# Scores in two buffers, masks half a row ahead, the transposed adjacency kept packed, x kept on chip

## The chip, the cores and the metric

The kernel runs on one core of a Trainium2 chip. TensorE (PE in the profile) multiplies and transposes, VectorE (DVE), ScalarE (ACT) and GpSimd (POOL) work elementwise, SyncE (SP) issues the transfers. The metric is the device time of one execution in microseconds.

## The reference

N = 4096 nodes, D = 128 features, `adj` is a 4096 x 4096 matrix of zeros and ones.

```python
deg = clip(adj.sum(axis=1), 1.0); dis = deg ** (-0.5)
diffusion = (dis[:, None] * adj * dis[None, :]) @ x - x
norms = maximum(norm(x, axis=-1), 1e-8)
sim = x @ x.T / (norms[:, None] * norms[None, :])
attn = softmax(beta * sim * adj, axis=1)
l0 = diffusion + sigmoid(alpha) * (attn @ x - x)
x = layernorm(x + l0)
x = layernorm(x + relu(adj @ (x @ weights)))
```

## The kernel before

All node indices are cut into R = 32 row blocks of 128 ("rows" below), and each row into C = 4 pieces of 1024 columns or H = 8 pieces of 512 columns ("steps" h = 0 to 7).

The attention stage handles one row after another. For row r, with q = r % 2:

- SP loads the row's adjacency in four pieces of 512 KB into `land`, which has two buffers (line 230). ACT casts each piece to bytes in `adj_bytes[q]`, with the row sums beside it (`cast`, line 369). The piece i is scaled by 64 >> i, so that POOL can add the four pieces into one `packed` block (`pack`, lines 287 to 293). PE turns it (`turn_adj`, line 838), and DVE takes it apart again by a shift and an AND, four instructions a row, into the row's transposed adjacency `adjT` of 128 KB a partition (`store_adj`, line 581).
- PE computes a row's cosines, three matmuls of 512 columns a step (`cosines`, line 853), into the two banks of `ps_s`. DVE multiplies them by the mask and writes `scores` (`mask`, line 593), with maxima beside it; `row_max` (lines 602, 604) makes the bias of the exponential. ACT computes the exponentials in place in four pieces (`exps`, line 401).
- PE turns the exponentials, four transposes a step, into one of four banks of `ps_e` (`turn_e`, line 864). ACT writes the high half in float16 (`e_high`, line 408), DVE the rest (`e_low`, line 608). PE multiplies both by x (`attend`, lines 877, 879), in `ps_acc`. DVE adds the finished row to `u` by two linked instructions (`attn_add`, lines 615, 618), after which `attend(r + 1, 0)` may start.

`scores` has one buffer. A mask of row r + 1 may be written at step h only once `turn_e(r, h)` has read it, so the masks of row r + 1 run beside the steps of row r, the last one at its step 7, and `row_max(r + 1)` and the exponentials of row r + 1 come after it. The order on each engine is written out by hand: on PE a step of row r is `turn_e(r, h)`, `attend(r, h - 3)`, `cosines(r + 1, h + 1)`, and the last three attends of a row stand behind its step 7, one of them in the next row. On DVE a step is `mask(r + 1, h)`, `e_low(r, h)`, then one of four `store_adj`, and `attn_add(r - 1)` stands at h = 2.

Between the stages x is loaded a second time from memory (line 247), POOL scales it by `dis` into `y` (lines 335, 339), and DVE writes the low halves (`y_low`, line 686).

The second stage has two layers of 32 rows. A row is 32 matmuls of 256 columns (line 918) with the transposed adjacency as weights, into one of four banks of `ps_e`. Rows 0 to 3 read `adjT` itself; the other rows read one of two buffers in `adj_bytes`, which `stage_block` fills two rows ahead by one copy of 128 x 1024 words (line 682). In layer 0, DVE's `step(r)` waits for the row's matmuls and then runs `stage_block`, `head0` (725, 728, 719, 721), `xw_low(r - 5)` (756) and `normalise(r - 1)` (745, 750). ACT's `step` runs `xw_high(r - 5)` (464), `turned_out(r - 4)` (458, 460) and `root(r)` (453), in that order. PE's `whole_row(r)` has `turn_x1(r - 4)` (924) in its middle and `x1_w(r - 4)` (929) behind it; the latter waits for line 460. Layer 1 has `head1` (735, 738) and `normalise` in its place, and no product with the weights.

## Time and profile before

| | us |
|---|---|
| median of 3 runs | 761.27 (760.44 to 761.53) |
| span of the profiled execution | 757.8 |
| attention stage and what stands ahead of it, until the first matmul of layer 0 | 518.17 |
| last matmul of layer 0 to the end | about 119 |

The profile is of one execution; its own device time is not stated, only its span, which lies 3.5 us below the median of the runs. The span begins with the first instruction. Durations in it overlap a little: an instruction of VectorE is shown some 0.08 us longer than the distance to the next one.

### The profile page before, as it was taken

How to read it: one execution, taken by the hardware profiler on the slowest of the kernel's cores; microseconds unless marked ns; L12 is line 12 of the kernel's file. 1: busy time of each engine (PE TensorE's matmuls, PEld its weight loads, DVE VectorE, ACT ScalarE, POOL GpSimd, SP SyncE). 2: the span in 40 equal slices, each digit the busy share in tenths (PEclk: the TensorE clock that was granted, in tenths of full speed). 3: DMA queues.
4: the chain of work that ended last, by engine and by line, in shares of the span. 5: the costliest groups of instructions: out<-in, count | busy, mean ns of one | idle time of the engine just before them, and what ended most of it. 6: DMA issues, size and time to landing. Idle time of an engine off the chain costs nothing. (4 is left out here: it accounts for less than half of the span.)

```text
span 757.8 us, 19379 instructions
## 1 busy us (share of the span) xinstructions
PE 721.4 (95%) x6163; PEld 578.5 (76%) x6163; DVE 572.1 (75%) x1644; ACT 494.4 (65%) x1001; POOL 128.7 (17%) x161
## 2 busy tenths in 40 slices
PE   6889989999999999999999999989999999999997
PEld 6567767777777777777777777768999998888886
DVE  4878878887888788878887888797566666465655
ACT  5888899889988998899889988982122223211111
POOL 2781112111211121112111211170000000000000
PEclk9999999999999999999999999999999999999999
DMA  5645543455445534553445345510000000000000
GB/s 177 189 139 143 159 132 124 127 152 160 115 129 151 160 114 131 150 159 115 130 150 159 115 131 149 169 51 5 1 0 0 0 0 0 12 17 14 28 14 28
DMA packets 22502, 73.81 MB, mean 97 GB/s; under 512 B 2640, under 2 KB 3152, under 8 KB 22480
## 3 DMA queue, kind: packets, MB, share of 16 engines
q1 hardware_dynamic: 22480, 73.54, 32.5%
q8 instruction: 11, 0.18, 0.1%
q14 instruction: 11, 0.09, 0.0%
HBM read 71.44 MB, written 2.10 MB: 97 GB/s over the span
## 5 line engine op out<-in xcount | busy, mean ns | idle before, releaser
L593 DVE CUSTOM_DVE_ANT_1 scores<-ps_s,adj_bytes 128x512 f32<-128x512 f32 x252 | 172.5, 685 | 72.7 <-PE ps_e L864 67.8
L853 PE MATMUL ps_s<-xn_parts,xn_signed 128*128 128x512 f16 x756 | 204.4, 380 | 1.7 <-DVE cmax L593 1.7
L877 PE MATMUL ps_acc<-x_parts,eT_parts 128*128 128x256 f16 x1024 | 192.8, 272 | 4.6 <-DVE u L618 2.0
L879 PE MATMUL ps_acc<-x_parts,eT_parts 128*128 128x128 f16 x1024 | 180.9, 219 | 0.0
L608 DVE SCALAR_TENSOR_TENSOR eT_parts<-ps_e,eT_parts 128x512 f16<-128x512 f32 x256 | 175.2, 685 | 3.7 <-ACT eT_parts L408 3.1
L864 PEld LDWEIGHTS ps_e<-ident,scores 128*128 128x128 f32 x1024 | 123.0, 141 | 69.7 <-issue 27.6
L408 ACT ACTIVATE eT_parts<-ps_e 128x512 f16<-128x512 f32 x256 | 147.0, 587 | 37.3 <-PE ps_e L864 36.6
L864 PE MATMUL ps_e<-ident,scores 128*128 128x128 f32 x1024 | 150.1, 274 | 18.4 <-ACT scores L401 18.4
L401 ACT ACTIVATE scores<-scores,col 128x1024 f32<-128x1024 f32 x128 | 157.6, 1231 | 1.1 <-DVE col L604 1.1
L369 ACT ACTIVATE adj_bytes<-land 128x1024 uint8<-128x1024 f32 x128 | 135.2, 1057 | 23.3 <-DMA land<-in_adj 22.7
L877 PEld LDWEIGHTS ps_acc<-x_parts,eT_parts 128*128 128x128 f16 x1024 | 100.0, 98 | 24.0 <-issue 9.6
L918 PE MATMUL ps_e<-xn_parts,adj_bytes 128*128 128x256 f16 x896 | 105.4, 273 | 0.0
L879 PEld LDWEIGHTS ps_acc<-x_parts,eT_parts 128*128 128x128 f16 x1024 | 100.1, 98 | 5.3
L918 PE MATMUL ps_e<-x_parts,adj_bytes 128*128 128x256 f16 x896 | 98.0, 273 | 0.0
L918 PEld LDWEIGHTS ps_e<-x_parts,adj_bytes 128*128 128x128 fp8e4 x896 | 87.7, 98 | 10.1
L918 PEld LDWEIGHTS ps_e<-xn_parts,adj_bytes 128*128 128x128 fp8e4 x896 | 87.7, 98 | 9.5
L853 PEld LDWEIGHTS ps_s<-xn_parts,xn_signed 128*128 128x128 f16 x756 | 60.2, 98 | 42.5 <-issue 2.1
L287 POOL TENSOR_TENSOR packed<-adj_bytes 128x256 uint32<-128x256 uint32 x32 | 23.3, 728 | 357.9 <-PE ps_at L838 357.9
L453 ACT ACTIVATE col<-mv,col 128x1 f32<-128x1 f32 x64 | 18.6, 291 | 97.7 <-DVE mv L721 97.7
L682 DVE COPY adj_bytes<-adjT 128x1024 uint32 (+1 forms) x56 | 38.8, 693 | 50.2 <-PE ps_e L918 50.2
L487 ACT ACTIVATE scores<-ps_e,col 128x128 f32<-128x128 f32 x32 | 11.8, 369 | 88.9 <-PE ps_e L918 88.9
L581 DVE TENSOR_SCALAR adjT<-ps_at 128x256 uint32 (+1 forms) x128 | 52.6, 413 | 0.0
(113 smaller groups left out, 570.1 us busy)
## 6 DMA issues: line engine op xcount, KB each, us to landing
land<-in_adj SPq DMA_DIRECT2D x128, 512.0 KB, 3.6
u<-in_x SPq DMA_DIRECT2D x4, 512.0 KB, 8.0
out<-u SPq DMA_DIRECT2D x7, 256.0 KB, 2.0
land<-in_x SPq DMA_DIRECT2D x2, 512.0 KB, 3.3
adj_bytes<-in_x SPq DMA_DIRECT2D x2, 512.0 KB, 3.8
out<-u SPq DMA_DIRECT2D x1, 192.0 KB, 1.9
eT_parts<-in_L_gnn_weights SPq DMA_DIRECT2D x1, 64.0 KB, 9.0
scores<-in_L_gnn_weights SPq DMA_DIRECT2D x1, 64.0 KB, 1.7
```

Of the source, the lines that this page charges most:

```text
L369: nc.scalar.activation(adj_bytes[:, q, i * CH:(i + 1) * CH], land[:, i % 2, :], ACT.Copy, scale=float(BYTE_ONE >> i), accum_out=deg[:, i, ...
L401: nc.scalar.activation(scores[:, i * CH:(i + 1) * CH], scores[:, i * CH:(i + 1) * CH], ACT.Exp, bias=neg_max, scale=abs_beta, accum_out=cs ...
L408: nc.scalar.activation(eT_parts[:, h % 4, 0, :], ps_e[:, h % 4, :], ACT.Copy, scale=E_SCALE).then_inc(e_hi, 1)
L581: nc.vector.tensor_scalar(adjT_rows[:, r, i * CH // K:(i + 1) * CH // K], ps_at[:, 0:CH // K].bitcast(U32), i, BYTE_ONE * 0x01010101, ALU. ...
L593: nc.vector.tensor_tensor_reduce(scores[:, o:o + BANK].rearrange("p (k q) -> p k q", k=K), score_bank(h, start).rearrange("p (k q) -> p k ...
L608: nc.vector.scalar_tensor_tensor(eT_parts[:, h % 4, 1, :], ps_e[:, h % 4, :], E_SCALE, eT_parts[:, h % 4, 0, :], ALU.mult, ALU.subtract).t ...
L682: nc.vector.tensor_copy(stage[q], adjT_rows[:, r, :]).then_inc(staged, 1)
L853: ins = nc.tensor.matmul(score_bank(h, start), xn_signed[:, q, part, :], xn_parts[:, other, o:o + BANK], start=(part == 0 and other == 0), ...
L864: ins = nc.tensor.transpose(ps_e[:, h % 4, n * P:(n + 1) * P], scores[:, t * P:(t + 1) * P], ident[:, :])
L877: nc.tensor.matmul(ps_acc[:, 0:2 * D], eT_parts[:, h % 4, 0, n * P:(n + 1) * P], x_parts[:, t, :], start=(t == 0), stop=(t == R - 1), skip ...
L879: ins = nc.tensor.matmul(ps_acc[:, 0:D], eT_parts[:, h % 4, 1, n * P:(n + 1) * P], x_parts[:, t, 0:D], start=False, stop=(t == R - 1), ski ...
L918: return nc.tensor.matmul(ps_e[:, n, 0:2 * D], lhs[:, b, :, k], y[t], start=(t == 0), stop=(t == R - 1))
```

## The change

- `scores`, `cmax`, `csum`, `neg_max` and `packed` get two buffers, `land` four.
- The masks of a row are made half a row earlier: steps 0 to 3 of row r make the masks 4 to 7 of row r + 1, with `row_max(r + 1)` at step 3, and steps 4 to 7 make the masks 0 to 3 of row r + 2. The cosines move with them, and in a step they stand ahead of `attend`. ACT makes the casts of row r + 2 in steps 0 to 3 and the exponentials of row r + 1 in steps 4 to 7. `attn_add(r - 1)` moves to h = 3. The last three attends of a row stand in steps 0 to 2 of the next.
- `store_adj` is one copy of the packed block into `packT`. `stage_block` takes the blocks apart in the second stage, by four instructions of 128 x 256 words a row, four rows ahead into a `stage` with four buffers, and now for all 64 rows.
- x is kept in `x_keep`; the second load is gone.

```diff
-        adjT = sb("adjT", [P, R, B, P], U32)
-        land = sb("land", [P, 2, CH], F32)
+        packT = sb("packT", [P, R, CH // K], U32)
+        stage = sb("stage", [P, G, N // K], U32)
+        land = sb("land", [P, C, CH], F32)
+        x_keep = sb("x_keep", [P, R, D], F32)
-        scores = sb("scores", [P, N], F32)
+        scores = sb("scores", [P, 2, N], F32)
...
-                sp.dma_start(x_again_at[q].rearrange("p (b k) d -> p b (k d)", b=2),
-                             x_v[:, 2 * q:2 * q + 2, :]).then_inc(x_again[q], 16)
...
             def row(r, q, start=False):
-                casts = (4, 5, 6, 7) if start else (3, 4, 6, 7)
-                exps(r, 0)
-                exps(r, 1)
...
+                for h in range(C):
                     e_high(r, h, start)
+                    cast(r + 2, q, h)
+                for h in range(C, H):
+                    e_high(r, h, start)
+                    exps(r + 1, 1 - q, h - C)
+
+            exps(0, 0, 0)
+            cast(1, 1, 2, first=True)
+            exps(0, 0, 1)
+            exps(0, 0, 2)
+            cast(1, 1, 3, first=True)
+            exps(0, 0, 3)
             row(0, 0, start=True)
...
+            def store_adj(r):
+
+                dve.wait_ge(adj_turned, r + 1)
+                nc.vector.tensor_copy(packT[:, r, :], ps_at[:, 0:CH // K].bitcast(U32)).then_inc(adj_stored, 1)
...
                 if not start:
-                    dve.wait_ge(e_turned, r * H + (h + 1 - H))
+                    dve.wait_ge(e_turned, r * H + (h + 1 - 2 * H))
...
-                    if h == 2 and not start:
+                    if h == 3 and not start:
                         if second:
                             dve.wait_ge(u_init, C)
                         attn_add(r - 1)
-                    mask(r + 1, 1 - q, h)
-                    if h == H - 1:
-                        row_max(r + 1)
+                    if h < C:
+                        mask(r + 1, 1 - q, h + C, start)
+                    elif not degrees:
+                        mask(r + 2, q, h - C)
+                    if h == C - 1:
+                        row_max(r + 1, 1 - q)
                     e_low(r, h)
-                    if h >= 4:
-                        store_adj(r, h - 4)
+                    if h == C:
+                        store_adj(r)
...
-                nc.vector.tensor_copy(stage[q], adjT_rows[:, r, :]).then_inc(staged, 1)
+            def stage_block(k, r, n):
+                for i in range(C):
+                    nc.vector.tensor_scalar(stage[:, n, i * CH // K:(i + 1) * CH // K], packT[:, r, :], i,
+                                            BYTE_ONE * 0x01010101, ALU.logical_shift_left,
+                                            ALU.bitwise_and).then_inc(staged, 1)
...
             for h in range(H):
-                if h == 2:
+                if h == 3:
                     attn_add(R - 2)
...
                 e_low(R - 1, h)
+                if h < C:
+                    stage_block(h, h, h)
+                if h >= C:
+                    y_low(h - C)
+                if h == C:
+                    store_adj(R - 1)
...
-            def step(r, n, lag, more=True):
+            def step(r, n, lag, ahead):
                 dve.wait_ge(rows_done, r + 1)
-                if lag >= G and more:
-                    stage_block(r + 2, n % 2)
+                stage_block(r + G, ahead, n)
                 head0(r, n)
...
-                step(r, r % G, 5, r + 2 < R)
-                if r + 2 >= R:
-                    stage_block(G + r + 2 - R, r % 2)
+                step(r, r % G, 5, r + G - R)
...
                 for h in range(H):
-                    turn_e(r, h, start)
+                    turn_e(r, q, h, start)
                     if h == 2:
-                        turn_adj(r, start)
+                        turn_adj(r, q, start)
+                    if h < C and left >= 1:
+                        cosines(r + 1, 1 - q, h + C)
+                    elif h >= C and left >= 2:
+                        cosines(r + 2, q, h - C)
                     if h >= LAG:
                         attend(r, h - LAG, start)
-                    elif h == 1 and not start:
-                        attend(r - 1, H - 1)
-                    if left and 1 <= h < H - 1:
-                        cosines(r + 1, 1 - q, h + 1)
-                for h in range(H - LAG, H - 1):
-                    attend(r, h, start)
-                    if left > 1:
-                        cosines(r + 2, q, h - (H - LAG))
+                    elif not start:
+                        attend(r - 1, h + H - LAG, second)
...
-                pe.wait_ge(staged, r + (layer * (R - G) - G + 1))
+                pe.wait_ge(staged, r * C + (layer * R * C + C))
```

## Rows read from the trace of the kernel before

**Rows 1.** The page, part 1: busy us (share of the span) x instructions.

```profile
PE 721.4 (95%) x6163; PEld 578.5 (76%) x6163; DVE 572.1 (75%) x1644; ACT 494.4 (65%) x1001; POOL 128.7 (17%) x161
```

**Rows 2.** Waits, 100 to 480 us: who waited for what: us, times, longest.

```profile
PEld ps_e L864 <- issue: 23.2, 25, 1.0
```

**Rows 3.** Timeline of VectorE: two of the 32 row maxima (start, us).

```profile
77.65 0.16 DVE L602 TENSOR_REDUCE col<-cmax 128x1 f32<-128x8 f32 x1
...
488.14 0.16 DVE L602 TENSOR_REDUCE col<-cmax 128x1 f32<-128x8 f32 x1
```

**Rows 4.** Timeline, 302.9 to 304.7 us: one step of PE, and ACT behind its transposes.

```profile
302.94 0.60 PE L864 MATMUL ps_e<-ident,scores 128*128 128x128 f32 x4
...
303.37 0.27 PE L877 MATMUL ps_acc<-x_parts,eT_parts 128*128 128x256 f16 x1
...
303.57 0.60 ACT L408 ACTIVATE eT_parts<-ps_e 128x512 f16<-128x512 f32 x1 [1.15 <-PE ps_e L864]
...
304.03 0.81 PE L853 MATMUL ps_s<-xn_parts,xn_signed 128*128 128x512 f16 x3
...
304.68 0.60 PE L864 MATMUL ps_e<-ident,scores 128*128 128x128 f32 x4
```

**Rows 5.** Timeline, 312 to 314 us: the sum of a row, and the attend behind it.

```profile
312.40 0.34 DVE L615 SCALAR_TENSOR_TENSOR u<-ps_acc,col,u 128x128 f32 x1
...
313.28 0.27 PE L877 MATMUL ps_acc<-x_parts,eT_parts 128*128 128x256 f16 x1
```

**Rows 6.** Timeline of ACT, about 300 to 310 us: high half, cast, exponential.

```profile
300.25 0.59 ACT L408 ACTIVATE eT_parts<-ps_e 128x512 f16<-128x512 f32 x1
...
300.73 1.05 ACT L369 ACTIVATE adj_bytes<-land 128x1024 uint8<-128x1024 f32 x1
...
308.76 1.23 ACT L401 ACTIVATE scores<-scores,col 128x1024 f32<-128x1024 f32 x1
```

**Rows 7.** Timeline of VectorE, 300 to 302 us: mask, low half.

```profile
300.45 0.68 DVE L593 CUSTOM_DVE_ANT_1 scores<-ps_s,adj_bytes 128x512 f32<-128x512 f32 x1
...
301.06 0.68 DVE L608 SCALAR_TENSOR_TENSOR eT_parts<-ps_e,eT_parts 128x512 f16<-128x512 f32 x1
```

**Rows 8.** Timeline: the first exponential, and the first matmul of attend(1, 0).

```profile
31.75 1.24 ACT L401 ACTIVATE scores<-scores,col 128x1024 f32<-128x1024 f32 x1 [0.31 <-DVE col L604]
```

```profile
54.20 0.27 PE L877 MATMUL ps_acc<-x_parts,eT_parts 128*128 128x256 f16 x1
```

**Rows 9.** The chain that ended last, the piece that begins layer 0.

```profile
518.17 15.83 PE ps_e L918 x145
```

**Rows 10.** Groups by line and form: table loads of ACT: busy us, mean ns.

```profile
L441 ACT ACT_TABLE_LOAD x2 | 2.6, 1283 | 0.0
```

**Rows 11.** Timeline of VectorE, 517 to 522 us: low half of y, four stores, two copies.

```profile
517.20 1.21 DVE L686 TENSOR_TENSOR xn_parts<-adj_bytes,xn_parts 128x1024 f16<-128x1024 f32 x1
...
518.98 1.41 DVE L581 TENSOR_SCALAR adjT<-ps_at 128x256 uint32<-128x256 uint32 x4
520.30 1.28 DVE L682 COPY adj_bytes<-adjT 128x1024 uint32<-128x1024 uint32 x2
```

**Rows 12.** Groups of VectorE by form: operations with pointers to scalars.

```profile
L604 DVE TENSOR_SCALAR col<-col 128x1 f32<-128x1 f32 x32 | 6.9, 214 | 1.1
...
L750 DVE TENSOR_SCALAR scores<-u,mv,rstd 128x128 f32<-128x128 f32 x12 | 4.2, 346 | 0.4
```

**Rows 13.** Waits of the whole span, in front of the copies of stage_block.

```profile
DVE adj_bytes L682 <- PE ps_e L918: 50.2, 52, 1.8
```

**Rows 14.** Timeline, 578 to 582 us: a row of layer 0.

```profile
578.00 0.69 DVE L682 COPY adj_bytes<-adjT 128x1024 uint32 x1 [0.93 <-PE ps_e L918]
...
581.04 0.27 ACT L460 ACTIVATE scores<-ps_s 128x128 f32<-128x128 f32 x1
...
581.50 0.39 PE L929 MATMUL ps_acc<-scores 128*128 128x128 f32 x2
```

**Rows 15.** Timeline, behind the last row of layer 0.

```profile
641.51 0.49 PE L929 MATMUL ps_acc<-scores 128*128 128x128 f32 x2 [0.27 <-ACT scores L460]
```

More of the change, by code:

```diff
@@ L99, in two_layer_gnn @@
         alpha_c, beta_c, e_alpha, sigma, u_scale, abs_beta = (c(n) for n in range(6))
-        neg_max, total, r_total, gain = (c(n) for n in range(6, 10))
+        neg_max = [c(6), c(29)]
+        total, r_total, gain = (c(n) for n in range(7, 10))
         attn_scale, x_up, dif_scale, w_up, w_down, eps_c = (c(n) for n in range(10, 16))
@@ L118, in two_layer_gnn @@
         w_loaded = sem("w_loaded")
[L119 to L120 removed]
+        land_full = [sem(f"land_full{i}") for i in range(C)]
         ident_zero = sem("ident_zero")
@@ L394, in _, with exps, e_high @@
             cast(1, 1, 1, first=True)
-            cast(1, 1, 2, first=True)
-            def exps(r, i):
+            def exps(r, q, i):
                 if i == 0:
                     act.wait_ge(max_done, r + 1)
-                nc.scalar.activation(scores[:, i * CH:(i + 1) * CH], scores[:, i * CH:(i + 1) * CH], ACT.Exp,
-                                     bias=neg_max, scale=abs_beta, accum_out=csum[:, i:i + 1]).then_inc(exp_done, 1)
-            def e_high(r, h, start):
+                piece = scores[:, q, i * CH:(i + 1) * CH]
+                nc.scalar.activation(piece, piece, ACT.Exp, bias=neg_max[q], scale=abs_beta,
+                                     accum_out=csum[:, q, i:i + 1]).then_inc(exp_done, 1)
+            def e_high(r, h, start=False):
                 act.wait_ge(e_turned, r * H + (h + 1))
@@ L447, in _ @@
                 row(r + 1, 1)
-            late_row(R - 2, 0)
-            late_row(R - 1, 1)
+            e_high(R - 2, 0)
+            e_high(R - 2, 1)
+            e_high(R - 2, 2)
+            act.wait_ge(deg_done, 1)
+            nc.scalar.activation(dis[:, :], dis[:, :], ACT.Sqrt).then_inc(deg_root, 1)
+            e_high(R - 2, 3)
+            nc.scalar.activation(table_loads[1], eps_c, ACT.Exp)
+            for h in range(C, H):
+                e_high(R - 2, h)
+                exps(R - 1, 1, h - C)
+            for h in range(H):
+                e_high(R - 1, h)
+                if h == 0:
+                    nc.scalar.activation(table_loads[2], eps_c, ACT.Sqrt)
             def root(r, q, base):
@@ L648, in _ @@
                                          ALU.mult, ALU.mult))
+            for h in range(C):
+                mask(1, 1, h, start=True)
             def row(r, q, start=False, second=False, degrees=False):
@@ L855, in cosines, with turn_e @@
                 ins.then_inc(s_done, 1)
-            def turn_e(r, h, start=False):
+            def turn_e(r, q, h, start=False):
                 if h % 2 == 0:
@@ L904, in _ @@
                 cosines(0, 0, h, start=True)
-            cosines(1, 1, 0)
-            cosines(1, 1, 1)
+            for h in range(C):
+                cosines(1, 1, h)
             row(0, 0, start=True)
-            row(1, 1)
+            row(1, 1, second=True)
             with pe.Fori(2, R - 3, 2) as r:
@@ L913, in _ @@
             row(R - 1, 1, left=0)
-            attend(R - 1, H - 1)
+            for h in range(H - LAG, H):
+                attend(R - 1, h)
             def add_tile(n, lhs, t, y):
```

204 lines of the change are left out of this document (78 added, 126 removed).

## The prediction

> **What bounds the kernel now.** I read the page first: PE is busy for 95% of the span [rows 1], and the chain that ended last consists of its matmuls in the second stage. That share says little of the attention stage, so I read next how long one of its rows takes. The maxima of 27 rows lie 410.5 us apart, 15.20 us a row [rows 3]. A step in which PE never stands takes 1.74 us: 0.43 for four transposes, 0.66 for eight attend matmuls, 0.65 for three cosines [rows 4]. Eight steps and the two transposes of the packed block (0.22, at a fourth of 0.43 each) make 14.14 us. So PE stands idle for 1.06 us in each row, and nearly all of that can be named. At the start of a row the weight loads of `turn_e` wait 0.93 us (23.2 over 25 rows, [rows 2]), because the exponentials cannot start before the last mask has been written. The rest lies mostly ahead of `attend(r, 0)`, behind `attn_add`. The second stage is PE's without holes: VectorE waits for PE 0.97 us in front of each staging copy [rows 13].
>
> **Scores in two buffers, masks and cosines half a row earlier.** The same instructions run, in another order, so only waits can change. The wait at the row's start goes: `exps(r + 1, 0)` now stands in step 4 of row r, and the transposes that need it are four steps later.
>
> Can ACT follow? In steps 4 to 7 it has a high half (0.48) and an exponential (1.23), 1.71 us against PE's 1.74; in steps 0 to 3 a high half and a cast, 1.53 us [rows 6, 4]. That makes 12.96 us of 14.14, just enough. The casts find their data: with four `land` buffers a piece is ordered a whole row ahead, and POOL packs long before.
>
> What is late next is `attn_add`, now at h = 3. I count from the start s2 of step 2. The cosines start behind six transposes, at s2 + 0.65, and their result is there after 0.81 and a few hundredths [rows 4], at s2 + 1.50. VectorE runs the mask (0.61) and the low half (0.60) [rows 7], until s2 + 2.71, and only then `attn_add`. From its first instruction to the attend behind it 0.88 us pass [rows 5]: `attend(r, 0)` can start at s2 + 3.59. PE gets to it at s2 + 1.96 + 0.43 + 0.65 = s2 + 3.04. So it waits 0.55 us in each row, and behind it on PE's queue everything else waits. Row: 14.14 + 0.55 = **14.69 us**, 0.51 less than now. Elsewhere VectorE has room: eight masks and low halves are 9.7 us [rows 7], the small instructions about 2.
>
> **Start.** ACT used to interleave the first row's exponentials with high halves. Now it does four exponentials and two casts first, from 31.75 [rows 8]: 4 x 1.23 + 2 x 1.05 = 7.0, so the first high half starts at 38.75. Four steps at 1.53 and four at 1.71 follow, 13.0 us, and row 1 begins on ACT at 51.7. The third high half of row 1 ends 3 x 0.48 + 2 x 1.05 later, at 55.2, its low half at 55.8, then `attn_add(0)`, and `attend(1, 0)` at 56.7, where it is at 54.20 now [rows 8]. That costs 2.5 us. This `attend` lies 7.07 us behind the start of its row (three steps with the 0.22, 1.08, the stall), so row 1 starts at 49.6 as PE sees it, and row 30 at 49.6 + 29 x 14.69 = 475.6.
>
> **Rows 30 and 31.** They lose cosines and masks, so PE is not the bound. In row 30 ACT passes its two table loads (1.3 us each with 0.2 of work, [rows 10]), starts the fifth high half at 8.7 (PE's step 4 begins at 8.1, and ACT follows 0.63 later, [rows 4]), and takes four times 1.71: row 31's first high half ends at 16.0. A third load: the second one ends at 18.0. From there VectorE bounds, as it carries the new staging and `y_low`: seven low halves 4.2, `attn_add` 0.76, three `y_low` at 1.13 (the next instruction overlaps the 1.21 by 0.08, [rows 11]) 3.4, the store and two small ones 0.6, and 12 staging instructions of pace p. Then PE's last attend, 0.8 with its signal. Layer 0 starts 27.8 + 12p behind row 30's start. The second load of x is off this path in either case: POOL needs some 13 us for y from the ninth microsecond of row 30 on, and `y_low(0)` comes at 24.
>
> **The pace p** is what the trace does not show: a shift and an AND from SBUF to SBUF. Bounds: the same operation from PSUM, four in 1.41 us, hence 0.33 apart [rows 11]; and the copy, which moves 1024 words in 0.69 us, faster than one word a cycle would allow (L686 needs 1.21 us for as many), and whose 0.59 pace for 1024 words gives 0.20 for 256 if the length-dependent 0.53 shrinks to 0.13 [rows 11]. The pointer operations speak for the slow end [rows 12]: one pointer and one element take 214 ns, two pointers and 128 elements 346, a full cycle for each element unless the second pointer costs 66 ns itself. I take 0.20, since source, target and number of inputs are the copy's, and keep 0.33. With it layer 0 starts at 475.6 + 30.2 = 505.8; with 0.33 at 507.4. Now it starts at 518.17 [rows 9]. Gain 12.4 or 10.8.
>
> The Trainium skill, VectorE: DVE Perf Modes, section "The TRN2 errata", speaks against cutting one copy into four: each instruction that reads SBUF pays a fixed cost, given as 58 cycles beside the elements. By its formula, an estimate, the copy costs 0.59 and four parts 0.78 at two elements a cycle, nearly my 0.80. Its tier table has tensor_scalar at two elements a cycle for fp32 in SBUF; rows 12 don't settle that for this operation.
>
> **Layer 0.** Staging takes 0.80 in place of 0.61, d = 0.19 (or 1.33, d = 0.72), at the head of VectorE's step. Its 0.93 us of idle time [rows 14] covers that as throughput. But behind it hang the statistics, `root`, `xw_high` and `turned_out` on ACT, and `x1_w` on PE. The copy of x1t ends at 581.31 and PE uses it at 581.50 [rows 14]; in the three other rows of a loop turn there are 0.5 us. Less a signal of 0.1, the slack is 0.1 once and 0.4 three times. A stall of one row gives the next the same time back, so about half of d minus slack remains as a mean: 0.6 us in all for p = 0.20, and (0.72 - 0.35) / 2 x 27 = 4.9 us for p = 0.33.
>
> **Between the layers.** PE already waits 0.27 us for this chain [rows 15]. In steps 30 and 31 the staging stood behind the rest, now it stands ahead: 0.80 (or 1.33) us on the path.
>
> **Layer 1.** The idle time of 0.97 [rows 13] covers d, rows are staged four ahead, and nothing on PE hangs on VectorE's answer. 0. The tail behind the last matmul has no staging before or after. 0.
>
> **Sum.** -12.4 + 0.6 + 0.8 = -11.0: span 746.8. The median of the runs lies 3.5 us above the profiled span, so **750.3 us**.
>
> **Rivals.**
> - *Slow staging* (p = 0.33): -10.8 + 4.9 + 1.3 = -4.6, 756.7 us. For it: rows 12.
> - *No stall at attn_add*: if VectorE reaches it earlier than I count, 29 x 0.55 = 16 us less, 734.3. Against it: every link of the chain is a measured duration and stands in a fixed order on VectorE's queue.
> - *VectorE takes the second stage, slower than before*: staging instructions with addresses from registers may not overlap at all. At the unoverlapped PSUM duration of 0.41 each, d is 1.04: last row 2.6 dearer (gain 9.8), layer 0 (1.04 - 0.32) / 2 x 27 = 9.7, between the layers 1.7, layer 1 0.06 x 27 = 1.6: +3.2, 764.5 us. It decides from p = 0.38 on, and at 0.5 VectorE alone would set both layers' rows.
> - *The new order gives nothing*: something I don't see (ACT, with 0.03 us to spare in a step) fills the row up to 15.20. 0.51 x 29 = 14.8 more: 765.1.
>
> **How the numbers follow.** Forecast 0.50, slow staging 0.23, no stall 0.09, VectorE-bound 0.12, nothing gained 0.06. The forecast's own range is 746 to 755 (0.1 us a row in the stall, 2 us at the start). The likeliest time is 750.3. The range runs from 738, between forecast and no stall, to 762, which holds slow staging and leaves out the two slow cases. A measurement tells 0.2%, 1.5 us, from no change. Slow staging may reach into that, so faster 0.80, same 0.07, slower 0.13.
>
> **What would show it.** Row maxima 14.7 us apart; PE's wait at a row's start gone and one of 0.55 ahead of `attend(r, 0)`, released by `attn_add`'s second instruction; `attend(1, 0)` at 56.7; layer 0 from about 506; staging instructions 0.20 apart and 0.29 long; PE waiting for x1t in layer 0 seldom, and 1.1 us between the layers. The forecast is wrong if the staging pace is 0.3 or more, or if rows are 14.2 or over 15.

## The result and the profile after

| | before | after |
|---|---|---|
| median of the runs, us | 760.34 (18 runs) | 762.27 (18 runs, 761.7 to 764.2) |
| span of the profiled execution, us | 757.8 | 760.1 |
| first matmul of layer 0, us | 518.17 | 518.50 |
| from there to the end, us | 239.6 | 241.6 |

The ratio is 1.003, with a 95% interval of 1.0021 to 1.0038: the change makes the kernel a little slower. The forecast was 750.3 us, with a range up to 762, and 11.0 us less span; 2.3 more came. The end of the attention stage hardly moved, so the missing gain has to be looked for there, row by row.

Each run with a span on record is 1.8 us longer than that span. The 3.5 us between span and median in the forecast were then these 1.8 and, an estimate, 1.7 by which the profiled execution was quicker than the median of three. So the spans miss the forecast by 13.3 us and the medians by 12.0; below, spans are compared.

Timeline of VectorE of the kernel after, three neighbouring row maxima (columns here and below: start us, duration us, engine, line, operation, out<-in, xcount, and in brackets the idle time before and who ended it; the lines that answer to [rows 3]):

```profile
446.62 0.16 DVE L586 TENSOR_REDUCE col<-cmax 128x1 f32<-128x8 f32 x1
...
461.66 0.16 DVE L586 TENSOR_REDUCE col<-cmax 128x1 f32<-128x8 f32 x1
...
476.70 0.16 DVE L586 TENSOR_REDUCE col<-cmax 128x1 f32<-128x8 f32 x1
```

They lie 15.04 us apart, where before had 15.20 and the forecast 14.69. In 29 rows that is 10.2 us of the 13.3 by which the forecast missed the span.

Waits of the kernel after, 100 to 480 us (who waited for whom: us in total, times, longest):

```profile
DVE scores L577 <- PE ps_s L839: 74.3, 151, 0.7
...
PE ps_acc L863 <- DVE u L602: 17.1, 26, 0.7
```

The wait of the weight loads at a row's start [rows 2] is gone. In its place PE waits 0.66 us in each row for the second instruction of `attn_add`. One row of VectorE shows why, and PE's attend behind it:

```profile
307.16 0.69 DVE L592 SCALAR_TENSOR_TENSOR eT_parts<-ps_e,eT_parts 128x512 f16<-128x512 f32 x1
308.57 0.69 DVE L577 CUSTOM_DVE_ANT_1 scores<-ps_s,adj_bytes 128x512 f32<-128x512 f32 x1 [0.73 <-PE ps_s L839]
309.19 0.08 DVE L577 DVE_READ_ACCUMULATOR2_ANT cmax<- 128x1 f32 x1
309.19 0.69 DVE L592 SCALAR_TENSOR_TENSOR eT_parts<-ps_e,eT_parts 128x512 f16<-128x512 f32 x1
309.79 0.34 DVE L599 SCALAR_TENSOR_TENSOR u<-ps_acc,col,u 128x128 f32 x1
310.17 0.35 DVE L602 SCALAR_TENSOR_TENSOR u<-ps_acc,col,u 128x128 f32 x1
```

```profile
310.67 0.27 PE L863 MATMUL ps_acc<-x_parts,eT_parts 128*128 128x256 f16 x1 [0.66 <-DVE u L602]
```

The cosines of this step began at 307.44. The mask on L577 starts 1.13 us behind that, the low half on L592 0.62 later, `attn_add` 0.60 later, and the attend another 0.88: 310.67. VectorE has nothing to do for 0.73 us ahead of that mask, and then is the late one.

Timeline of the last row of the kernel after, VectorE's first three staging blocks (a block is four instructions), and POOL beside them:

```profile
500.44 3.88 DVE L670 TENSOR_SCALAR stage<-packT 128x256 uint32<-128x256 uint32 x4
...
504.83 1.20 DVE L670 TENSOR_SCALAR stage<-packT 128x256 uint32<-128x256 uint32 x4
...
506.56 0.88 DVE L670 TENSOR_SCALAR stage<-packT 128x256 uint32<-128x256 uint32 x4
```

```profile
499.12 1.90 POOL L327 TENSOR_TENSOR x_keep<-x_keep,norm_r 128x1024 f32<-128x1024 f32 x1
501.11 1.17 POOL L330 TENSOR_SCALAR xn_parts<-x_keep 128x1024 f16<-128x1024 f32 x1
502.24 1.92 POOL L327 TENSOR_TENSOR x_keep<-x_keep,norm_r 128x1024 f32<-128x1024 f32 x1
```

Four staging instructions take 0.88 us where they are alone, and 3.88 in the first block, beside POOL's work on y. One by one, the first, third and fourth instruction of that block are:

```profile
500.44 0.73 DVE L670 TENSOR_SCALAR stage<-packT 128x256 uint32<-128x256 uint32 x1
...
501.29 1.12 DVE L670 TENSOR_SCALAR stage<-packT 128x256 uint32<-128x256 uint32 x1
...
502.34 1.98 DVE L670 TENSOR_SCALAR stage<-packT 128x256 uint32<-128x256 uint32 x1
```

They end at 501.17, 502.41 and 504.32, each 0.15 us behind the end of one of POOL's three instructions (501.02, 502.28, 504.16). The one-input conversion on L330 holds VectorE up just as the two multiplications do. The low half at 499.83, whose first input is in PSUM, takes its usual 0.69 beside the first of the multiplications.

`attn_add(30)` stands behind three of these blocks on VectorE's queue, and PE waits for it for 8 us, in which the granted clock falls:

```profile
508.23 0.37 PE L863 MATMUL ps_acc<-x_parts,eT_parts 128*128 128x256 f16 x1 [8.03 <-DVE u L602]
```

Table by stretch of the kernel after (stretch, length, busy us of each engine with the number of instructions, granted clock as a share of full speed, then the share of the DMA engines and GB/s):

```profile
490.00:500.00 10.00, 9.53 (x101) 8.59 (x99) 6.47 (x20) 9.74 (x18) 6.69 (x5) 1.00 0.01 2
500.00:510.00 10.00, 1.97 (x13) 1.53 (x12) 9.46 (x22) 2.69 (x5) 5.12 (x4) 0.64 0.00 0
510.00:520.00 10.00, 9.40 (x87) 8.22 (x86) 8.37 (x14) 2.39 (x4) 0.00 (x0) 0.85 0.03 8
```

The second stage is close to what was forecast. Between the layers [rows 15] became:

```profile
643.82 0.49 PE L912 MATMUL ps_acc<-scores 128*128 128x128 f32 x2 [1.08 <-ACT scores L447]
```

From the first matmul of layer 0 to this one 125.32 us pass, 123.34 before: 0.81 of the difference is the wait, and 1.17 lie in layer 0. From here to the end it is 116.3 us in both.

### The profile page after: what moved, and what is told of

It is laid out like the page before. It is cut to its first block, busy times and chain, and to the rows that moved or that the text cites. A ratio compares the mean times of both kernels' runs of the same rounds, so it can differ in the third digit from the quotient of the medians.

```text
span 760.1 us, 19535 instructions
## 1 busy us (share of the span) xinstructions
PE 716.8 (94%) x6163; PEld 577.6 (76%) x6163; DVE 568.1 (75%) x1748; ACT 499.5 (66%) x1001; POOL 128.2 (17%) x161
## 4 chain that ended last, share of the span: by engine, by line
PE 84%; DVE 9%; ACT 3%; issue 3%; DMA 1%; DVEq 0%; SPq 0%; ACTq 0%
PE ps_e L901 29%; PE ps_s L839 17%; PE ps_acc L863 14%; PE ps_e L850 12%; PE ps_acc L865 7%; DVE eT_parts L592 3%; DVE u L602 1%; DVE u L599 1%; ACT scores L392 1%; ACT adj_bytes L360 1%; DVE stage L670 1%; ACT eT_parts L399 1%; PE ps_at L823 1%; DMA x_keep<-in_x 1%; PE ps_acc L912 1%
## 5 line engine op out<-in xcount | busy, mean ns | idle before, releaser
L577 DVE CUSTOM_DVE_ANT_1 scores<-ps_s,adj_bytes 128x512 f32<-128x512 f32 x252 | 173.9, 691 | 87.1 <-PE ps_s L839 82.8
L399 ACT ACTIVATE eT_parts<-ps_e 128x512 f16<-128x512 f32 x256 | 152.5, 596 | 53.8 <-PE ps_e L850 46.8
L592 DVE SCALAR_TENSOR_TENSOR eT_parts<-ps_e,eT_parts 128x512 f16<-128x512 f32 x256 | 175.4, 685 | 9.3 <-ACT eT_parts L399 9.1
L863 PEld LDWEIGHTS ps_acc<-x_parts,eT_parts 128*128 128x128 f16 x1024 | 100.5, 98 | 77.1 <-DVE eT_parts L592 34.7
L850 PE MATMUL ps_e<-ident,scores 128*128 128x128 f32 x1024 | 156.2, 275 | 0.0
L901 PE MATMUL ps_e<-xn_parts,stage 128*128 128x256 f16 x1024 | 119.4, 273 | 0.3
L901 PE MATMUL ps_e<-x_parts,stage 128*128 128x256 f16 x1024 | 113.0, 273 | 0.0
L850 PEld LDWEIGHTS ps_e<-ident,scores 128*128 128x128 f32 x1024 | 108.8, 142 | 3.7
L901 PEld LDWEIGHTS ps_e<-x_parts,stage 128*128 128x128 fp8e4 x1024 | 100.2, 98 | 11.5
L901 PEld LDWEIGHTS ps_e<-xn_parts,stage 128*128 128x128 fp8e4 x1024 | 99.7, 98 | 12.1 <-issue 1.1
L839 PEld LDWEIGHTS ps_s<-xn_parts,xn_signed 128*128 128x128 f16 x756 | 73.6, 98 | 38.4 <-DVE cmax L577 4.3
L670 DVE TENSOR_SCALAR stage<-packT 128x256 uint32 (+1 forms) x256 | 60.7, 300 | 44.5 <-PE ps_e L901 44.5
L269 POOL TENSOR_TENSOR xn_signed<-xn_parts,col 128x256 f16<-128x256 f32 (+1 forms) x32 | 19.6, 613 | 317.3 <-PE ps_s L839 317.3
```

The costliest lines, as they stand in the source:

```text
L399: nc.scalar.activation(eT_parts[:, h % 4, 0, :], ps_e[:, h % 4, :], ACT.Copy, scale=E_SCALE).then_inc(e_hi, 1)
L577: nc.vector.tensor_tensor_reduce(scores[:, q, o:o + BANK].rearrange("p (k q) -> p k q", k=K), score_bank(h, r == 0 if start else False).re ...
L592: nc.vector.scalar_tensor_tensor(eT_parts[:, h % 4, 1, :], ps_e[:, h % 4, :], E_SCALE, eT_parts[:, h % 4, 0, :], ALU.mult, ALU.subtract).t ...
L670: nc.vector.tensor_scalar(stage[:, n, i * CH // K:(i + 1) * CH // K], packT[:, r, :], i, BYTE_ONE * 0x01010101, ALU.logical_shift_left, AL ...
L839: ins = nc.tensor.matmul(score_bank(h, start), xn_signed[:, q, part, :], xn_parts[:, other, o:o + BANK], start=(part == 0 and other == 0), ...
L850: ins = nc.tensor.transpose(ps_e[:, h % 4, n * P:(n + 1) * P], scores[:, q, t * P:(t + 1) * P], ident[:, :])
```

## The experiments

All edits are made to the kernel after, only e7's to the kernel before. "Row" is the distance of two row maxima, as a mean. "Layer 0 at" is the start of its first matmul.

| kernel | median us | ratio to before (95%) | span | row | layer 0 at |
|---|---|---|---|---|---|
| after | 762.27 | 1.003 (1.0021 to 1.0038) | 760.1 | 15.04 | 518.50 |
| e1, the mask's wait for PE last | 758.42 | 0.998 (0.9966 to 0.9993) | 756.4 | 14.87 | 514.88 |
| e2, attn_add ahead of the mask | 745.93 | 0.9815 (0.9796 to 0.9834) | 744.6 | 14.43 | 503.05 |
| e5, both | 744.68 | 0.9783 (0.9754 to 0.9812) | 743.0 | 14.38 | 501.46 |
| e3, row 31: low halves ahead of staging | 759.2 | 0.9985 (0.9971 to 1.0) | 757.4 | 15.04 | 515.02 |
| e4, y begins behind three stagings | 761.8 | 1.0028 (1.0014 to 1.0043) | 760.0 | 15.04 | 518.46 |
| e8, e3 and 32 products | 760.37 | 1.0 (0.9982 to 1.0018) | 759.7 | 15.04 | 517.29 |
| e10, e3 and 16 products | 757.11 | 1.0002 (0.9985 to 1.0018) | 755.6 | 15.04 | 513.14 |
| e7, before with packing alone | 762.96 | 1.0028 (1.0004 to 1.0051) | 762.3 | 15.22 | 519.93 |
| e6, all together | 741.0 | 0.9737 (0.9708 to 0.9765) | 738.1 | 14.38 | 497.22 |
| e9, e6 with 10 products | 739.84 | 0.9767 (0.9741 to 0.9792) | 737.2 | 14.38 | 496.19 |

Beside e9 and e10 the kernel before ran in 756.8 us, beside the others in 760.2 to 760.4, so their ratios do not compare with the others to the third digit. Their stretches are compared in the traces. The start differs too: the first row maximum lies anywhere from 29.4 to 31.4 us, so last rows are compared by the distance from row 31's maximum to layer 0.

**The row, e1: which of the mask's waits comes last on its queue.** The mask waits for three signals. PE's, which comes last in time, stood first.

```diff
-                dve.wait_ge(s_done, r * H + (h + 1))
                 if not start:
                     dve.wait_ge(e_turned, r * H + (h + 1 - 2 * H))
                 dve.wait_ge(cast_done, r * C + (h // 2 + 1))
+                dve.wait_ge(s_done, r * H + (h + 1))
```

> The changed kernel, with one edit: in `mask` VectorE waits for the cosines (`s_done`) last, behind its waits for `e_turned` and `cast_done`, and not first. Those two have long been met, so the data are ready at the same moment. In the changed kernel a mask starts 1.13 us behind the start of its three cosine matmuls, where the forecast took 0.85, and `attend(r, 0)` starts 0.82 us late where it took 0.55. Theory (VectorE's queue works off each of the two later waits, with values from registers, only once the cosines' signal has come): the mask starts at 0.85, the stall shrinks by 0.28 to about 0.55, a row takes 14.77 in place of 15.04, and the span falls by 29 x 0.28 = 8 us, to 752. Rival (the signal of a 512-column matmul group itself comes 0.3 us behind the end that the profile shows): mask at 1.13, row 15.04, span 760 as before.

Timeline, the same step, with the cosines at 305.87:

```profile
305.87 0.81 PE L839 MATMUL ps_s<-xn_parts,xn_signed 128*128 128x512 f16 x3
...
306.82 0.69 DVE L577 CUSTOM_DVE_ANT_1 scores<-ps_s,adj_bytes 128x512 f32<-128x512 f32 x1 [0.67 <-PE ps_s L839]
...
308.91 0.27 PE L863 MATMUL ps_acc<-x_parts,eT_parts 128*128 128x256 f16 x1 [0.48 <-DVE u L602]
```

The mask now starts 0.95 us behind the cosines' start instead of 1.13, and the row is 0.17 shorter. So 0.18 of the 0.28 us that I had left out were two waits that VectorE still had to work through after PE's signal, 0.09 each. The other 0.10 stayed: that much later than the "few hundredths" of the forecast the mask starts even so. The theory had put all of the 0.28 down to the waits, and so the span at 752. It is 756.4: 29 rows give 5.1 us, and this execution's first exponential started 1.2 us later than in after.

**The row, e2: `attn_add` earlier.**

```diff
-                    if h == 3 and not start:
+                    if h == 2 and not start:
+                        e_low(r, h)
                         if second:
                             dve.wait_ge(u_init, C)
                         attn_add(r - 1)
...
-                    e_low(r, h)
+                    if h != 2 or start:
+                        e_low(r, h)
```

> The changed kernel, with one edit: at h = 2 VectorE runs `e_low(r, 2)`, then `attn_add(r - 1)`, then the mask, in place of mask, low half and, at h = 3, the sum. Theory (what makes a row longer than PE's 14.2 us is only the place of `attn_add` on VectorE's queue): the sum starts as soon as attend(r - 1, 7) is done, about 0.1 us behind the start of PE's step 3, `attend(r, 0)` 0.88 us later, which is before PE gets to it at 1.08. The stall of 0.82 goes, a row takes 14.22 to 14.3 us, and 29 rows give 22 to 24 us: span 736 to 738. Rival (ACT, with 12.96 us of work a row in a fixed order against PE's steps, or the masks now made later, take the row up again): row 14.7 or more, span 750 or more, with a new wait of PE behind ACT or behind a mask.

Timeline of VectorE:

```profile
314.55 0.69 DVE L592 SCALAR_TENSOR_TENSOR eT_parts<-ps_e,eT_parts 128x512 f16<-128x512 f32 x1 [0.29 <-ACT eT_parts L399]
315.58 0.35 DVE L599 SCALAR_TENSOR_TENSOR u<-ps_acc,col,u 128x128 f32 x1 [0.34 <-PE ps_acc L867]
315.97 0.35 DVE L602 SCALAR_TENSOR_TENSOR u<-ps_acc,col,u 128x128 f32 x1
316.34 0.69 DVE L577 CUSTOM_DVE_ANT_1 scores<-ps_s,adj_bytes 128x512 f32<-128x512 f32 x1
```

`attn_add` now waits for PE (L867 is the last attend of the row before) and not for the mask. The row is 14.43 us, 0.61 less than in after, and the whole kernel is 1.85% faster than before. What is left over eight steps of 1.75 and the two turns of the packed block (14.22) is 0.21, where 0 to 0.1 was expected. The rest lies at the old place: the sum starts 0.41 us behind PE's step 3 (315.17 to 315.58) and not 0.1, and with the 0.88 to the attend that is 1.29, where PE is ready after 1.08. PE's cosines of that step, 0.65 long elsewhere, are followed by `attend(r, 0)` after 0.85 to 0.86 us in each row from 65 to 440 us.

The span was expected at 736 to 738 and is 744.6. From the first row maximum to the last it is 17.2 us less than in after, not 22 to 24, and this execution's first maximum came 1.8 us later. In the last row nothing was changed, and PE waited there as in after:

```profile
492.86 0.37 PE L865 MATMUL ps_acc<-x_parts,eT_parts 128*128 128x256 f16 x1 [8.45 <-DVE u L602]
```

**The row, e5: both, and the wait order of `attn_add` too.**

```diff
-                dve.wait_ge(attn_part, r * H + H)
                 dve.wait_ge(total_done, 3 * r + 3)
+                dve.wait_ge(attn_part, r * H + H)
```

> The kernel with the sum first (e2), with two more edits: in `mask` the wait for the cosines is the last one, and in `attn_add` the wait for `attn_part` comes behind that for `total_done`. In e2 a row takes 14.43 us, PE's own work is 14.22, and `attn_add` starts 0.3 us behind the end of the last attend. Theory (of what VectorE's queue adds to a signal, about 0.09 us is due to each wait that stands behind it, as 0.18 for two in e1): `attn_add` starts 0.09 earlier, the row falls to 14.34, span 742. Rival (the waits' order cost something only where a mask was the late one, and e2's rest is the signal alone): row 14.43, span 744.6.

Timeline of VectorE, `attn_add` of two neighbouring rows:

```profile
314.40 0.35 DVE L599 SCALAR_TENSOR_TENSOR u<-ps_acc,col,u 128x128 f32 x1 [0.32 <-PE ps_acc L867]
...
328.75 0.35 DVE L599 SCALAR_TENSOR_TENSOR u<-ps_acc,col,u 128x128 f32 x1 [0.25 <-PE ps_acc L867]
```

Theory and rival each hold for half of the rows: they take 14.34 and 14.41 us by turns, 14.38 as a mean, for 14.43 in e2. In one row `attn_add` starts 0.45 us behind the start of the last attend, in the next 0.38; in e2 it was 0.47 to 0.48. So the wait moved ahead gives its 0.09 in every second row and 0.02 in the others. Why the rows differ was not found.

**The last row, e3: the low halves of row 31 ahead of its staging.**

```diff
                 e_low(R - 1, h)
-                if h < C:
-                    stage_block(h, h, h)
-                if h >= C:
-                    y_low(h - C)
...
+            stage_block(0, 0, 0)
+            for q in range(C):
+                y_low(q)
+            for h in range(1, C):
+                stage_block(h, h, h)
             attn_add(R - 1)
```

> The changed kernel, with one edit: in row 31 VectorE runs all eight low halves with `attn_add(30)` and the small steps first, and only then the first staging block, the four low halves of y, and the three other staging blocks. In the changed kernel layer 0 starts 34.7 us behind row 30, the forecast was 30.2; four staging instructions took 3.88 us there, and PE waited 8.0 us for `attn_add(30)`, behind them. Theory (the loss is the staging ahead of `attn_add(30)` on VectorE's queue, made longer by GpSimd's work on y at the same time): PE's wait falls under 3 us, its clock is not lowered, staging instructions take 0.2 each as GpSimd has finished, and layer 0 starts 4 to 7 us earlier, span 753 to 756. Rival (VectorE's sum of work bounds these rows in any order): layer 0 starts within 1.5 us of where it did, span 759 or more.

```profile
504.13 0.37 PE L864 MATMUL ps_acc<-x_parts,eT_parts 128*128 128x256 f16 x1 [3.63 <-DVE u L602]
```

PE's wait fell from 8.03 to 3.63 us, but layer 0 starts only 3.8 us closer to row 31's maximum (23.22 for 27.00), and the span is 757.4 and not 753 to 756. The clock was 0.66 of full speed from 500 to 510 us all the same, and the last row was now paced by hand-overs from PE to ACT (below). The edit does three things at once: `attn_add(30)` comes earlier, no staging meets POOL any more, and blocks 1 to 3 run from 518.2 us on, behind the first matmul of layer 0 at 515.02. So the 3.8 us are not the price of one of them.

**The last row, e4: is it POOL that holds up the staging?** POOL's third and fourth piece of y wait until three blocks are staged.

```diff
+                if q == 2:
+                    pool.wait_ge(staged, 3 * C)
                 y_q = x_keep[:, q * TC:(q + 1) * TC, :]
```

> The changed kernel, with one edit: GpSimd waits for three staging blocks of row 31 before it works on the third and fourth quarter of y. Nothing waits for these quarters until 10 us later. Theory (a two-input operation of GpSimd and VectorE's staging from SBUF to SBUF exclude each other, so that the one waits for the other's end): the first staging block takes 0.9 us in place of 3.88, the second 0.9 in place of 1.20, and layer 0 starts some 3 us earlier, span 757. Rival (the first block is slow because its instructions run for the first time, or because the adjacency copy of row 30 is late): it takes 3.9 us again, span 760.

Timeline of VectorE and of POOL:

```profile
501.49 0.89 DVE L672 TENSOR_SCALAR stage<-packT 128x256 uint32<-128x256 uint32 x4
...
506.88 4.11 DVE L672 TENSOR_SCALAR stage<-packT 128x256 uint32<-128x256 uint32 x4
```

```profile
505.80 1.90 POOL L329 TENSOR_TENSOR x_keep<-x_keep,norm_r 128x1024 f32<-128x1024 f32 x1 [5.59 <-DVE stage L672]
507.78 1.17 POOL L332 TENSOR_SCALAR xn_parts<-x_keep 128x1024 f16<-128x1024 f32 x1
508.92 1.92 POOL L329 TENSOR_TENSOR x_keep<-x_keep,norm_r 128x1024 f32<-128x1024 f32 x1
```

The slow block moved with POOL: blocks 0 to 2 took 0.89 each, block 3, beside POOL, 4.11. So it is the neighbour, not the place in the program. Of the 3 us that were expected, 1.1 came: from row 31's maximum (492.55) to layer 0 (518.46) it is 25.91 us for 27.00 in after. Layer 0 still began at the same time, because this execution's maxima lie 1.05 us later. PE's wait for `attn_add(30)` fell from 8.03 to 5.25 us, but the same 3.2 us were lost again in block 3, which stands ahead of the last low halves.

**The clock, e8 and e10: PE kept at work through its wait.** Products of the identity with itself, into a bank of `ps_s` that nobody reads any more, are extra work and change no result.

```diff
+                    if left == 0 and h == LAG:
+                        for _ in range(32):
+                            nc.tensor.matmul(ps_s[:, 0, 0:P], ident[:, :], ident[:, :], start=True, stop=True)
                     if h >= LAG:
                         attend(r, h - LAG, start)
```

> The kernel with row 31's low halves first (e3), with 32 products of the identity with itself added on PE in row 31, into a bank that nobody reads, ahead of its wait for `attn_add(30)`. They fill a wait of 3.6 us. In e3 the granted clock is 0.66 from 500 to 510 us, and a high half comes 1.1 to 2.5 us late behind PE's transposes. Theory (PE's clock falls to its lower level in that wait, and the chain of transposes, high halves and low halves behind it is slow for that reason): the clock stays at 1.0, and layer 0 is reached 1 to 2.5 us earlier, span 755 to 756.4. Rival (the chain is bound by the hand-overs between PE, ACT and VectorE, whatever the clock): span 757.4, or a little more for the products themselves.

The 32 products were 64 matmuls in the trace and took 7.15 us. The first attend came at 509.16, 3.5 us behind the end of `attn_add(30)`, where it is 0.15 in e10; so they ran 3.35 us over the wait. They did hold the clock at 1.00. As the two effects lay on top of each other, e10 took 16.

> The kernel with the last row's low halves ahead of its staging, with 16 identity products instead of 32 ahead of the last row's first attend: 3.6 us, from 502.0 to about 505.6, which is when attn_add(30) ends. Without products TensorE waited 3.63 us there, the clock was 0.66 in 500 to 510, the high halves 4 to 7 took 5.04 us from the first to the last, and layer 0 began at 515.02; with 32 products the clock was 1.00, they took 3.30 us, but layer 0 began at 517.29 because the products ran 3.7 us over the wait. Theory (the lower clock on the last row's turns costs 1.7 us, and the overshoot cost the other kernel 3.7 us): the clock stays near 1.00, the high halves take about 3.3 us, and layer 0 begins at 515.0 - 1.7 = 513.3, a span of 755.4 to 756. Rival (the pace of the last row is ScalarE's and VectorE's, and the clock costs nothing on the path): layer 0 begins at 515 again and the span is 757 to 758.

Timelines of ACT, high halves 4 to 7 of row 31, first e3, then e10:

```profile
506.46 0.60 ACT L399 ACTIVATE eT_parts<-ps_e 128x512 f16<-128x512 f32 x1 [3.47 <-PE ps_e L851]
508.60 0.60 ACT L399 ACTIVATE eT_parts<-ps_e 128x512 f16<-128x512 f32 x1 [1.54 <-PE ps_e L851]
510.39 0.60 ACT L399 ACTIVATE eT_parts<-ps_e 128x512 f16<-128x512 f32 x1 [1.20 <-PE ps_e L851]
511.50 0.60 ACT L399 ACTIVATE eT_parts<-ps_e 128x512 f16<-128x512 f32 x1 [0.51 <-PE ps_e L851]
```

```profile
506.31 0.60 ACT L399 ACTIVATE eT_parts<-ps_e 128x512 f16<-128x512 f32 x1 [2.44 <-PE ps_e L851]
507.41 0.60 ACT L399 ACTIVATE eT_parts<-ps_e 128x512 f16<-128x512 f32 x1 [0.51 <-PE ps_e L851]
508.51 0.60 ACT L399 ACTIVATE eT_parts<-ps_e 128x512 f16<-128x512 f32 x1 [0.51 <-PE ps_e L851]
509.61 0.60 ACT L399 ACTIVATE eT_parts<-ps_e 128x512 f16<-128x512 f32 x1 [0.51 <-PE ps_e L851]
```

In e3 ACT waits 1.54 and 1.20 us for PE's transposes while the clock is low, in e10 0.51 each time: 5.04 us from the first to the last against 3.30. Layer 0 began at 513.14, forecast 513.3. Counted from row 31's maximum (491.80 and 492.67) it is 23.22 against 20.47: the lower clock cost this row 2.75 us, 1.74 of them between these high halves and 1.0 ahead of them. The first attend stands 12.3 us behind the maximum in both.

**The packing alone, e7.** To the kernel before only `packT`, the four-instruction staging and its place four rows ahead were added; the order of the attention stage stayed.

```diff
-            def stage_block(r, q):
-
-                nc.vector.tensor_copy(stage[q], adjT_rows[:, r, :]).then_inc(staged, 1)
+            def stage_block(k, r, n):
+                for i in range(C):
+                    nc.vector.tensor_scalar(stage[:, n, i * CH // K:(i + 1) * CH // K], packT[:, r, :], i,
+                                            BYTE_ONE * 0x01010101, ALU.logical_shift_left,
+                                            ALU.bitwise_and).then_inc(staged, 1)
```

> The kernel before, with one part of the change alone: the transposed adjacency is kept packed (one copy a row), and taken apart in the second stage by four instructions a row into four buffers, four rows ahead. One buffer of scores, the old order of masks, and the second load of x stay; the staging blocks of rows 0 to 3 stand around the last `y_low`. Theory (this part costs only what the forecast gave it: 0.6 us in layer 0, 0.8 between the layers, and here four blocks of 0.8 us less the four stores and two copies they replace, some 1 to 3 us ahead of or in the first rows of layer 0): rows of the attention stage stay at 15.20 us, layer 0 and 1 together take 1.5 to 2.5 us longer than before, span 760 to 762. Rival (three stores a row fewer on VectorE also shorten the attention rows, or the staging is dearer than in the forecast): rows under 15.1 us and span under 757, or the second stage over 3 us longer.

Rows are 15.22 us, for 15.20 before. The second stage is 762.3 - 519.93 = 242.4 us for 239.6, 2.8 more where 1.5 to 2.5 was expected and after has 2.0. Between the layers stands the same 1.08 us as in after:

```profile
646.05 0.49 PE L923 MATMUL ps_acc<-scores 128*128 128x128 f32 x2 [1.08 <-ACT scores L457]
```

So the packing by itself costs 0.28% (0.04 to 0.51). The new order of the attention stage had to earn that back, and as it was written out it did not: after and e7 have the same ratio within their intervals. Its rows are 0.16 us shorter than before's, 4.6 us over 29 rows, yet layer 0 starts at 518.50 for 518.17: the new start and rows 30 and 31 took that back.

**All together, e6 and e9.** e5, and in row 31: low halves 0 to 3 with `attn_add(30)`, then two stagings, then low halves and `y_low` by turns, the last two stagings behind; ACT's table load behind the fourth high half; 32 products; in the last two steps of layer 0 the staging behind the rest again, as before had it.

```diff
-                if h < C:
-                    stage_block(h, h, h)
+                if h == 3:
+                    stage_block(0, 0, 0)
+                    stage_block(1, 1, 1)
...
+            stage_block(2, 2, 2)
             attn_add(R - 1)
+            stage_block(3, 3, 3)
```

> All edits together on the changed kernel: the sum ahead of the mask at h = 2, the signal waited for last in `mask` and `attn_add`, in row 31 the low halves 0 to 3 first, then two staging blocks, then low halves and `y_low` by turns, the other two blocks at the end, ACT's last table load behind its fourth high half, 32 products of the identity on PE in its wait, and in the last two steps of layer 0 the staging behind the other work. Theory: 742 for the rows (14.34 us each), 4 to 6 us less in rows 30 and 31, 0.8 us less between the layers: span 736 to 738, about 3% under the kernel before. Rival (the gains at the end overlap: PE cannot start layer 0 before VectorE has done its 15 us there): span 740 or more.

The span is 738.1, at the upper end of what was expected. The second stage is 240.9 us, 0.7 less than in after, and PE waits 0.27 us between the layers again, so the 0.81 more in after were the place of the staging:

```profile
621.81 0.49 PE L923 MATMUL ps_acc<-scores 128*128 128x128 f32 x2 [0.27 <-ACT scores L447]
```

e9 is e6 with `range(10)`.

> The kernel with every reordering put together, with 10 identity products instead of 32 ahead of the last row's first attend. The 32 took 7.15 us (481.24 to 488.39) where attn_add(30) had ended at 483.52, so they held TensorE 4.9 us too long. Ten take 10 x 0.223 = 2.2 us and end at 483.5, just as attn_add(30) does. Theory (the products' overshoot was on the path): what stands behind them comes up to 4.9 us earlier, less what VectorE then adds, since its staging of two blocks keeps it until 487.95 and the second group of low halves waited only 2.20 us for ScalarE: 2.2 to 4.9 us, so a span of 733.2 to 735.9 and a median of 736 to 739, a ratio near 0.970. The granted clock stays at 1.00 in the slices around 480 to 490. Rival (VectorE and ScalarE set the end of the last row, and the overshoot lay beside their work): the span stays within 1 us of 738.1.

Timelines of PE (e9), then VectorE (e9):

```profile
482.32 2.40 PE L889 MATMUL ps_s<-ident 128*128 128x128 f32 x20
484.92 0.27 PE L871 MATMUL ps_acc<-x_parts,eT_parts 128*128 128x256 f16 x1 [0.20 <-DVE u L602]
```

```profile
485.28 3.92 DVE L672 TENSOR_SCALAR stage<-packT 128x256 uint32<-128x256 uint32 x8
489.13 0.68 DVE L592 SCALAR_TENSOR_TENSOR eT_parts<-ps_e,eT_parts 128x512 f16<-128x512 f32 x1
```

From row 31's maximum to layer 0 it is 21.91 us in e9 (474.28 to 496.19) and 24.18 in e6 (473.04 to 497.22): 2.27 less, at the lower end of the 2.2 to 4.9 expected, because VectorE now goes on without a hole from its staging (eight instructions in 3.92, again beside POOL) to the low half on L592. The attention stage of e9 began 1.24 us later, so its span is only 0.9 less than e6's. Both versions are over 2% faster than before and after.

## Why the prediction was wrong

**Where it was right.** The wait at the row's start went away and the new one stood where it was put, ahead of `attend(r, 0)`, released by the second instruction of `attn_add`. The start: from the first exponential to `attend(1, 0)` 25.02 us (29.86 to 54.88), forecast 24.95 (31.75 to 56.7). That the absolute time came out 1.8 us better is the first exponential's start, 1.9 earlier than in [rows 8]; the start differs by as much between other runs here. The pace p: four in 0.88, 0.30 long, 0.20 apart, as taken. By the rule of the Trainium skill, VectorE: DVE Perf Modes, section "The TRN2 errata", the estimate was 0.78 for the four, beside a measured pace of 0.80; the trace agrees where nothing disturbs them. Between the layers: 0.81, forecast 0.80. Layer 1: 0, as forecast. Layer 0: 1.17 for 0.6, a small miss of the term.

The prediction named rows over 15 us as a sign that it is wrong, and they take 15.04.

**Where it failed first: the start of the mask.** The step reads: the cosines' "result is there after 0.81 and a few hundredths", so 0.85 in all. It was 1.13. The 0.04 for a signal came from nothing in the trace; e1 showed 0.09 for each of two waits that stood behind the signal on VectorE's queue, and 0.10 that stays with the signal itself. So the term was 0.28 us too small, while all other links, 0.62, 0.60 and 0.88, were right. 0.28 us in a chain that is 0.55 late turn it into 0.82 late, and a step of 1.75 in place of 1.74 adds 0.08 over eight: 14.69 + 0.27 + 0.08 = 15.04. Between 60 and 480 us the trace of before has no mask that waited for its cosines, so this link had to be bounded, and a neighbour was at hand: in [rows 4] ACT starts 0.63 behind transposes of 0.43, 0.20 for PE's signal to another engine. With it the result is there at s2 + 0.65 + 1.01 and the stall is 0.71, not 0.55; only the waits in the queue would have been missed.

**What the term was worth.** The forecast took a gain of 0.51 us a row and had 0.1 us a row of margin for the one new dependence that it stood on. The two rivals with no gain, 764.5 and 765.1, came nearest to 762.27. The first was not at work: VectorE kept the staging pace of 0.20. The second is true in its general half: something unseen filled the row, to 15.04 of its 15.20. But it was not ACT, which it names, and it gives no account of the last row. That its figure is near is luck.

**Where it failed second: the last row.** The step reads "From there VectorE bounds", and counts 12 staging instructions at pace p = 0.20 behind row 31's second high half, the first block done before it. Counted from row 30's first transposes at 483.8, layer 0 comes after 34.7 us and not 30.2. Up to that high half the sum holds: it ends 17.9 us behind them, forecast 18.0. Then VectorE's trace shows where the time went.
- The first block is not done before it. It takes 3.88 us beside POOL, so the second low half starts at 504.23 and not at 501.8: 2.4 us.
- The second block takes 1.20 for 0.88, for the same reason: 0.3 us.
- VectorE, which should have had no hole, waits 1.70 us for ACT ahead of the low half at 511.19. ACT waits for PE, and PE for `attn_add(30)`, which stands behind three blocks on VectorE's queue, and then runs at the lower clock.

That makes 4.4 us. e4 shows that the slow block moves with POOL, and that without it PE's wait is 5.25 us and not 8.03; e3's order brings it to 3.63. The forecast named POOL only for whether its y would be in time, and not for what it does to VectorE. What the clock can cost is shown by e3 and e10: 2.75 us behind a shorter wait, in an order that leaves VectorE less to do ahead of layer 0.

**The balance of the span.** The start gave -1.8. The rows from `attend(1, 0)` at 54.88 to `attend(30, 0)` at 491.01 gave +10.1. From there to layer 0 it is 27.5 us for 23.1, +4.4, and the second stage gave +0.6 (its 2.0 for 1.4). That makes the 13.3 measured.

Two sums of the prediction are a little off by its own terms. PE's step 4 of row 30 comes 7.7 us behind the row's start and not 8.1 (7.9 was measured), and the stalls of layer 0 under slow staging make 5.0 and not 4.9. Neither changes the account.

**What stays open.** It was not found why e5's earlier wait gives its 0.09 us only in every second row. What the clock cost in after itself, behind its 8 us wait, was not run; by VectorE's trace it is part of the 1.70. The 0.8 us by which e7's second stage is longer than that of after was not traced.

## What to carry to other kernels

If a change trades one wait for another, the gain is the difference of two nearly equal chains: take every link of the new chain, signals and the waits queued behind them included, from the same pair of engines in the trace, and ask what 0.1 us more at each of them does. Put the wait that is fulfilled last at the end of its list, and put short instructions that release another engine (here `attn_add`) ahead of long ones that nobody waits for. Where a loop ends, walk through each engine's queue in order instead of adding durations: a sum of VectorE's work cannot show that another engine waits for something in its middle. And ask of each instruction on such a path which other engine works beside it there: a pace measured alone need not hold beside a neighbour.

## What the hardware showed

- VectorE's shift and AND from SBUF to SBUF, 128 x 256 words, runs at 0.20 us each, and four take 0.88 to 0.90 alone. Beside POOL four of them took 3.88 (after) and 4.11 us (e4), and eight took 3.92 (e9). In these three runs each of the nine staging instructions that were held up ended 0.15 us behind the end of an instruction of POOL, one-input or two-input. The Trainium skill, GPSIMD Engine Reference, section "Specifications", says that GpSimd's SBUF interfaces are shared with VectorE, with contention when VectorE's instructions run in a 2-port mode or have two SBUF inputs; the runs fit that, and low halves, with one input in PSUM, kept their 0.69 us.
- A wait that is already fulfilled, but stands behind the one VectorE is held at, costs 0.09 us after the signal: 0.18 for the mask's two (e1), 0.09 and 0.02 by turns for the one of `attn_add` (e5).
- From the start of a group of 512-column matmuls that the profile shows as 0.81 us to the start of VectorE's instruction that waits for it last, 0.95 us pass (e1).
- Behind 8.03 us in which PE stood, the granted clock in the 10 us around it was 0.64; behind 3.63 us it was 0.66, and 1.00 when products filled the wait. The two levels are 2.4 and 1.2 GHz, so both slices were partly at the lower one.
- A product of two float32 tiles of 128 x 128 appears as two matmuls and takes 0.22 to 0.24 us; the float32 transposes of the kernel appear as one each, four in 0.43.
